# Half of the out-projection moved into the last chunk of the scan, the rest into the first iterations of the next phase, with the last two FFN contributions an iteration later

## What is computed

```python
xz = x @ W_in + b_in                        # 512 -> 2 x 1024
u, z = silu(xz[:, :1024]), xz[:, 1024:]
B, C = split(u @ W_xproj + b_xproj)         # 16 states each
dt = softplus(u @ W_dt + b_dt)
h = h * exp(dt * A) + dt * u * B;  y = sum_states(h * C) + D_param * u   # scan over time
o = (y * silu(z)) @ W_out + b_out           # the out-projection, 1024 -> 512
x = layernorm(x + o)
q = x @ wq.T + bq;  k, v from ctx (77 tokens);  16 heads of 32
x = layernorm(x + softmax(mask(q k / sqrt(32))) @ v @ wo.T + bo)
hidden = x @ W1 + b1                        # 512 -> 2048
a = relu(hidden + gain * sin(theta + 0.1 * hidden))
x = layernorm(x + a @ W2 + b2)
```

## Time and profile before

| what | value |
|---|---|
| median of 3 runs | 3416.74 us (3415.76 to 3419.22) |
| the profiled execution | 3416.91 us, span 3415.2 us |
| PE busy | 2934.8 us, 86% of the span |
| DVE busy | 2738.8 us, 80% |
| ACT busy | 1999.3 us, 59% |
| POOL busy | 1777.3 us, 52% |
| mean granted TensorE clock | 0.940 |

### The profile page before, as it was taken

How to read it: one execution, slowest core, us unless ns; L and a number is a source line. 1 busy time by engine, 2 the same in 40 slices (tenths; PEclk the granted TensorE clock), 3 DMA queues, 4 the chain that set the end, 5 groups by cost and what they waited for, 6 DMA issues and landing times. The chain is left out here.

```text
span 3415.2 us, 49521 instructions
## 1 busy us (share of the span) xinstructions
PE 2934.8 (86%) x18996; PEld 1318.5 (39%) x18996; DVE 2738.8 (80%) x3098; ACT 1999.3 (59%) x3570; POOL 1777.3 (52%) x893
## 2 busy tenths in 40 slices
PE   5888879889889888798897849999999999999997
PEld 2222222222222222222221236666666666666664
DVE  3999999999999999999999966666666666666664
ACT  4776776677667667766775444444444444444444
POOL 3797988978888879889788611111111111111100
PEclk8999999999999999999997769999999999999999
DMA  4111111111111111111113140000000000000000
GB/s 144 50 47 59 48 55 41 47 59 47 35 59 53 47 61 47 54 41 47 59 41 112 34 150 8 26 26 25 25 25 25 26 26 25 25 25 25 25 7 13
DMA packets 92547, 153.66 MB, mean 45 GB/s; under 512 B 12002, under 2 KB 29026, under 8 KB 91875
## 3 DMA queue, kind: packets, MB, share of 16 engines
q1 hardware_dynamic: 92386, 151.54, 14.0%
HBM read 92.79 MB, written 58.72 MB: 44 GB/s over the span
## 5 line engine op out<-in xcount | busy, mean ns | idle before, releaser
L722 POOL TENSOR_TENSOR h<-h,c_rep 128x1024 f32<-128x1024 f32 x512 | 1198.3, 2355 | 309.4 <-ACT carry L532 308.7
L655 DVE TENSOR_TENSOR_SCAN h<-r_ps,carry,h 128x512 f32<-128x512 f32 x768 | 942.8, 1272 | 7.2 <-ACT r_ps L526 6.5
L526 ACT ACTIVATE r_ps<-r_ps,decay 128x512 f32<-128x512 f32 x1024 | 632.0, 656 | 334.0 <-PE r_ps L295 333.3
L642 DVE TENSOR_TENSOR h<-u_ps,b_rep 128x1024 f32<-128x1024 f32 x512 | 618.7, 1208 | 44.3 <-PE u_ps L306 43.5
L1524 POOL TENSOR_TENSOR x<-x,rows 128x1024 f32<-128x1024 f32 x32 | 76.4, 2388 | 975.8 <-PE tr L961 975.8
L306 PE MATMUL u_ps<-dtu,spread 32*128 32x512 f16 x2048 | 326.6, 398 | 110.5 <-DVE h L642 109.4
L295 PE MATMUL r_ps<-dt,spread 32*128 32x512 f16 x2048 | 324.5, 396 | 75.5 <-DVE h L655 62.7
L318 PE MATMUL y_ps<-h,gather 128*32 128x512 f32 x2048 | 297.6, 650 | 55.6 <-POOL h L722 55.6
L655 DVE TENSOR_TENSOR_SCAN h<-r_ps,zero,h 128x512 f32<-128x512 f32 x256 | 313.9, 1269 | 6.9 <-ACT r_ps L526 6.7
L40 PE MATMUL nat<-region,act 128*128 128x512 f16 x512 | 206.8, 404 | 94.5 <-DVE act L1378 48.4
L40 PE MATMUL fps<-x,region 128*128 128x256 f16 x1024 | 280.9, 274 | 3.8 <-issue 2.4
(11 more groups left out here) (222 smaller groups left out, 5653.8 us busy)
## 6 DMA issues: line engine op xcount, KB each, us to landing
u_t_dram<-u SPq DMA_DIRECT2D x16, 1024.0 KB, 4.9
z_t_dram<-zs SPq DMA_DIRECT2D x32, 512.0 KB, 3.0
uz<-u_t_dram SPq DMA_DIRECT2D x64, 256.0 KB, 3.8
uz<-z_t_dram SPq DMA_DIRECT2D x64, 256.0 KB, 4.2
y_t_dram<-y SPq DMA_DIRECT2D x64, 256.0 KB, 2.4
y_t<-y_t_dram SPq DMA_DIRECT2D x15, 1024.0 KB, 7.5
x_in<-dram_x SPq DMA_DIRECT2D x16, 512.0 KB, 8.1
result<-x SPq DMA_DIRECT2D x16, 512.0 KB, 3.4
```

The source lines that it names most:

```text
L526: nc.scalar.activation(bank, bank, ACT.Exp, scale=decay[:, col:col + 1]).then_inc(s_da, 1)
L642: nc.vector.tensor_tensor(h[:, g % H_GROUPS, o:o + 2, :], u_ps[:, :, :], b_rep[:, c % 2:c % 2 + 1, :].broadcast_to([P, 2, TS]), ALU.mult). ...
L655: nc.vector.tensor_tensor_scan(row, r_ps[:, 2 * (pair % 2) + o, :], row, start, ALU.mult, ALU.add)\
L722: nc.gpsimd.tensor_tensor(rows, rows, c_rep[:, c % 2:c % 2 + 1, :].broadcast_to([P, 2, TS]), ALU.mult)\
```

## The change

**In the scan phase.** Between pairs 18 and 30 of the last chunk `W_out` is loaded and split, into the part of `region` that the u half of `W_in` has left. From pair 26 on, 16 tiles of `y_t` (tokens 0 to 2047, which were stored long before) are loaded, split, multiplied and stored to a new DRAM tensor `o`: `y_high` on ACT every second pair, `y_low` on POOL every pair, `out_piece` on PE in pairs 28 to 59, one half tile (12 matmuls of 512 columns) a pair, `evacuate_out` on ACT every second pair. The keys and values move to pairs 60 to 63.

**In the second phase.** The body takes `x1 = x + o + b_out` from DRAM loads and two POOL additions (`x1_sum`, for the next chunk), and normalizes it in the iteration before. Chunks 8 to 15 are projected here: three in iteration 0, one in each of the iterations 1 to 5, tile by tile through one `y_t` buffer, evacuated by ACT and stored to `o`. `second(6)` and `second(7)` of a chunk, its residual, layernorm and store come an iteration later (`late`), around the transposes of `x1`; so there is one body more at the end. Then come the transposes of `x2` and the queries, ahead of `hidden(0)`. The scores alternate between two lanes from matmul to matmul. POOL's `x2_bias` waits for the scores of the first tile, and `x1_sum` comes behind it. `front_back` is now called `body`, and `softmax_b` `probabilities`. The region of the split `W_1` and `W_2` is exchanged, and there are ten weight pieces to split in this phase, not twelve. Below: SP's tile loads and their places, PE's half tile, POOL's part, and the order of the bodies.

```diff
-KV_AT = (40, 42, 44, 46)
+KV_AT = (60, 61, 62, 63)
+OUT_TILES = 16
+W_OUT_AT, OUT_AT = 18, 28
...
+            def load_y_tile(i):
+                g = i % 4
+                if i < 4:
+                    sp.wait_ge(s_wol, 2 * i + 2)
+                else:
+                    sp.wait_ge(s_yl, 2 * (i - 3))
+                for r in range(2):
+                    sp.dma_start(w_out_raw[:, 2 * g + r, :].rearrange("p (q t) -> p q t", q=4),
+                                 a["y_t"].rearrange("(j p) t -> p j t", p=P)[:, 4 * r:4 * r + 4, i * P:(i + 1) * P])\
+                        .then_inc(s_yraw[g], 16)
...
+                for i in range(OUT_TILES):
+                    if s == min(W_OUT_AT + 4 + 2 * i, 62):
+                        load_y_tile(i)
+                    if s == min(OUT_AT + 2 + 2 * i, 63):
+                        store_out_tile(i)
...
+            def out_piece(i, part):
+                if part == 0:
+                    pe.wait_ge(s_oe, i) if i else pe.wait_ge(s_ev, NC * PIECES)
+                pe.wait_ge(s_yl, 2 * i + part + 1)
+                for k in range(4 * part, 4 * part + 4):
+                    tokens = slice(k % 4 * P, k % 4 * P + P)
+                    last = split_product(nc, pj[:, :], [y16[s][:, i % 4, part, tokens] for s in range(2)],
+                                         [w_out[s][:, k, :] for s in range(2)], k == 0, k == NJ - 1)
...
+                if W_OUT_AT + 2 <= s < W_OUT_AT + 2 + NJ:
+                    w_out_low(s - W_OUT_AT - 2)
+                if OUT_AT - 2 <= s < OUT_AT - 2 + 2 * OUT_TILES:
+                    y_low((s - OUT_AT + 2) // 2, s % 2)
...
+OPS_FIRST, OPS_UNTIL = 3, 6
...
+            body(0, 0, 0, True, False, False, range(OPS_FIRST), True)
+            body(1, 1, 0, True, True, False, one(1), True)
+            for c in range(2, PER_BATCH, 2):
+                two(c, 0, one if c < OPS_UNTIL else lambda c: ())
+            with e.Fori(PER_BATCH // 2, CHUNKS // 2 - 1) as h:
+                two(2 * h, 1, lambda c: ())
+            body(CHUNKS - 2, 0, 1, True, True, True, (), True)
+            body(CHUNKS - 1, 1, 1, True, True, True, (), False)
+            body(CHUNKS, 0, 1, False, True, True, (), False)
+            body(CHUNKS + 1, 1, 1, False, False, True, (), False)
```

The new body of PE (its beginning), of POOL (whole), and a piece of DVE's, in this order; ACT's order follows DVE's:

```diff
+            def body(c, par, batch, front, back, late, ops, more):
+                b, d = c - 1, c - 2
+                if late:
+                    second(d, 6)
+                if front:
+                    x1_transposed(c, par, back)
+                if late:
+                    second(d, 7)
+                if back:
+                    x2_transposed(c, par)
+                if front:
+                    queries(c)
+                if back:
+                    hidden(b, 0)
+                for m in ops:
+                    out_projection(c, m, 0)
+                    out_projection(c, m, 1)
+                if back:
+                    hidden(b, 1)
+                if front:
+                    scores(c, 0, batch, (0, 1), ops)
...
+            def body(c, par, batch, front, back, late, ops, more):
+                for m in ops:
+                    for t in range(NT):
+                        y_low(m * NT + t, t)
+                if front:
+                    x1_bias(c, par)
+                if back:
+                    pool.wait_ge(s_scp, b_scores(c, front))
+                    x2_bias(c - 1, 1 - par)
+                if more:
+                    x1_sum(c + 1, 1 - par)
...
+                if back:
                     fraction(b, 0)
+                if front:
+                    masked(c, 0, (0, 1))
+                if back:
                     fraction(b, 1)
                     mix(b, 0)
+                if front:
+                    masked(c, 0, (2, 3))
+                if back:
                     fraction(b, 2)
                     act_low(b, 0)
+                    mix(b, 1)
+                if front:
+                    row_maximum(c, 0)
+                    masked(c, 1, (0, 1))
```

More of the change, by code:

```diff
@@ L981, in hidden, with second, scores @@
                     last.then_inc(s_hp, 1)
-            def scores(c, t, batch, lanes):
+            def second(b, n, tiles=range(NT)):
+                if n == 0:
+                    pe.wait_ge(s_wlo, W2_SPLIT)
+                    pe.wait_ge(s_rw2, b * NT)
+                pe.wait_ge(s_actl, b * NU + n + 1)
+                for t in tiles:
+                    last = natural(nat[:, t, :], act16, w_2, NF, t, 2 * n, 2 * n + 2)
+                    if n == NU - 1:
+                        last.then_inc(s_w2, 1)
+            def scores(c, t, batch, lanes, ops):
                 for lane in lanes:
@@ L1078, in front_back @@
                     hidden(b, 5)
-                if front:
-                    scores(c, 1, batch, (2, 3))
-                if back:
+                    second(b, 2)
+                    hidden(b, 6)
                     second(b, 3)
-                    hidden(b, 6)
-                    second(b, 4)
-                    hidden(b, 7)
                 if front:
@@ L1458, in front_back @@
                 if back:
-                    mix(b, 1)
+                    act_low(b, 1)
                     fraction(b, 3)
-                    act_low(b, 1)
                     mix(b, 2)
+                if front:
+                    masked(c, 1, (2, 3))
+                    less_maximum(c, 0)
+                if back:
+                    act_low(b, 2)
                     mix(b, 3)
-                    act_low(b, 2)
+                if front:
+                    row_maximum(c, 1)
+                if back:
+                    fraction(b, 4)
@@ L1478, in front_back @@
                 if front:
-                    masked(c, 1, (2, 3))
-                    row_maximum(c, 1)
+                    probabilities(c, 0)
                 if back:
+                    act_low(b, 4)
                     fraction(b, 5)
-                    act_low(b, 4)
+                if front and not back:
+                    weights_low(6)
+                if more:
+                    statistics("x1", 0, c + 1, x1[:, 1 - par, :, :])
                 if front:
-                    less_maximum(c, 1)
@@ new lines, in _, with body @@
+            pool.wait_ge(s_rows, 3 * 16)
+            x1_sum(0, 0)
+            def body(c, par, batch, front, back, late, ops, more):
+                for m in ops:
+                    for t in range(NT):
+                        y_low(m * NT + t, t)
+                if front:
+                    x1_bias(c, par)
+                if back:
+                    pool.wait_ge(s_scp, b_scores(c, front))
+                    x2_bias(c - 1, 1 - par)
+                if more:
+                    x1_sum(c + 1, 1 - par)
```

736 lines of the change are left out of this document (404 added, 332 removed).

## The result

The changed kernel takes 3498.26 us (median of 4 runs, 3496.99 to 3500.74), the kernel before 3416.76 in the same comparison (4 runs): a ratio of 1.0238, with a 95% interval of 1.0221 to 1.0256. The change made the kernel 2.4% slower. The profiled execution took 3497.45 us, with a span of 3495.7, 80.5 more than before.

A forecast was written before the change was run, and what follows sets the result against it. It took DVE to bound the scan and PE the steady iteration. Its terms, +15 + 41 + 5.5 + 36 - 14 - 2 = +81.5 us on 3416.9, gave 3498 us, with a range of 3400 to 3550.

The forecast's parts named there:

- (d): Steady iteration: POOL's three operations alternate with DVE's, act_low(0) 5.8 us late, two PE waits; 84 us against 85.4.
- rival C: Steady iteration: POOL's three operations cost DVE nothing; iteration 76.5 us, total 3386; chance 0.17.
- the sentence that the prediction cited: Trainium skill on GpSimd: it contends with VectorE's instructions with two SBUF inputs or in a two-port mode.
- (c): Prologue and iteration 0: three chunks projected through one y_t buffer, 129 us in place of 88; +41, bounds +25 and +50.
- (b): Scan: added out-projection on PE, POOL's lag, and late keys and values; +15 us, bounds +4 and +35.
- POOL's lag: Scan, pairs 20 to 28: POOL has 43 us to do in 32; 5 us taken of the 11.
- (e): Iterations 1 to 5: out-projection adds 10.4 us each; +5.5 for the first, +9 for each of four.
- Iterations 6 to 15: Ten second-phase iterations without out-projection, each 1.4 us shorter than before; -14 us.
- B: Steady iteration: DVE keeps the port between operations, act_low(0) 3.6 us late; iteration 80.5, total 3446; chance 0.15.
- E: Scan becomes PE's or POOL's, tile loads late, PE's clock drops; +50 there, total 3530 to 3590; chance 0.12.
- D: Steady iteration: PE stays the bound, DVE's order costs nothing; iteration 68 us, total 3258; chance 0.04.

The follow-up runs named there:

- e1_pool_early: Changed kernel with POOL's x2_bias no longer waiting for the scores of the first tile: 3390.94 us.
- e7_one_pool_op_small: Changed kernel with POOL's addition of the out-projection's bias done for 16 of 512 columns of each row: 3470.66 us.
- e4_w_out_low_small: Changed kernel with POOL's eight w_out_low subtractions in the last scan chunk done for 16 of 512 columns each: 3497.69 us.
- e12_lows_small: Changed kernel with POOL's w_out_low and its y_low of the first four tiles done for 16 of 512 columns: 3500.53 us.
- e9_keys_values_quarter: Changed kernel with one of four contraction tiles in each keys_values step at pairs 60 to 63: 3497.44 us.
- e10_quarters_early: Changed kernel, POOL without its wait, ACT copying all four quarters of the first tile's transposed probabilities earlier, DVE's next-chunk statistics later: 3346.78 us.
- e2_probs_out_early: Changed kernel with ACT copying the first two quarters of the first tile's transposed probabilities right behind exps(c,1): 3490.74 us.
- e5_both_waits: Changed kernel with the edits of e1_pool_early and e2_probs_out_early together: 3384.6 us.
- e6_two_first: e5_both_waits with two chunks' out-projection in iteration 0 in place of three, the other six in iterations 1 to 6: 3385.81 us.

## Why the prediction was right, and where it was not

It said 3498.0 us, and 3498.26 came out. The mechanism of the steady iteration, which decides the sign, holds. That the numbers meet to 0.3 us is luck: the scan and iterations 1 to 5 came 20 us longer than predicted, and the other parts 21 us shorter.

**The iteration (d).** Right in the step that it turns on, and in the sum. Three POOL operations back to back after the fourth group of scores; they and DVE's three alternate; `act_low(0)` 5.7 us late, against 5.8 predicted; PE's wait before `second(b,0)` 5.68 us and a second one of 6.76 before the third quarter of the transposes, against 6 and 6; 83.3 to 83.9 us, against 84. Behind the last scores two slips cancel. From the last masks to the end of `fraction(6)` DVE takes 21.8 us (from 2902.64 to the end of the row below), where the prediction counted 19.2 with two `mix`, two `fraction` and no normalization of `x1`; the trace has three of each and that normalization:

```profile
2923.71 0.69 DVE L1517 TENSOR_TENSOR units<-units 128x512 f32<-128x512 f32 x1
```

From there to the end of `w_o` it is 18.4 us, where 20 and 2 for the clock were allowed. The cause of the first wait is shown by taking it away (in e1_pool_early the iteration fell to 75.1 to 76.5; rival C had 76.5 and a total of 3386, measured 3390.94) and by taking a third of it away (e7_one_pool_op_small). The changed kernel has a control of its own, though not a clean one. Iteration 15 has no next chunk, so `x2_bias` stands alone: one DVE instruction is held, PE waits 1.5 us, and the iteration takes 75.3. The next chunk's statistics and normalization are missing there as well, and the second wait is 4.1 in place of 6.8; in e1_pool_early iteration 15 is 1.4 us shorter than the one before it.
The Trainium skill (SBUF — State Buffer, Who interferes with whom) goes further than the sentence that the prediction cited: whichever of GpSimd and VectorE, with two SBUF inputs or in a two-port mode, issues first holds the shared ports for its whole instruction, and the other is fully blocked. By this rule, the traces agree: a mask instruction of 0.24 us took 2.39 in e1_pool_early. Whose turn comes next at a boundary it doesn't say; here the two alternate.

**Prologue and iteration 0 (c).** 40.2 us against 41. POOL's timeline has the first, second, third and last of the six tiles' `y_low` (the phase begins at 2002.0, as the prediction had begun it at 1974):

```profile
2036.59 2.12 POOL L1717 TENSOR_TENSOR y<-y_t,y 128x1024 f16<-128x1024 f32 x1 [19.22 <-ACT y L1308]
2043.91 2.12 POOL L1717 TENSOR_TENSOR y<-y_t,y 128x1024 f16<-128x1024 f32 x1 [5.21 <-ACT y L1308]
2054.90 3.28 POOL L1717 TENSOR_TENSOR y<-y_t,y 128x1024 f16<-128x1024 f32 x1 [8.86 <-ACT y L1308]
...
2083.25 2.13 POOL L1717 TENSOR_TENSOR y<-y_t,y 128x1024 f16<-128x1024 f32 x1 [5.26 <-ACT y L1308]
```

The first ends 36.7 us into the phase (36 predicted); then they end 7.3 to 7.7 and 12 us apart in turn, where the prediction had 9 and 11. The last matmul is at 89 (90).

**The scan (b).** The step that was mis-sized: +15, measured +27.8, inside its bounds of 4 and 35. The prediction gave POOL's lag 5 us of the 11 that it had counted, for the three groups of `h` were to take up the rest; the block in which it lies lost 12.1. POOL's work was counted rightly: from pair 20 to 28 the trace has 43.4 us (43 predicted), and the scan took 43.6 for it, in place of the 32 expected. About 4.5 of the 12.1 go with POOL's added work (e4_w_out_low_small, e12_lows_small). The rest, as far as the traces show, is a chain through PE: the piece that waits for POOL stands ahead of the next pair's replication, and after the wait it runs at half clock. The 2.6 us of the block before are a term that the prediction put at nothing: ACT's part of splitting `W_out`, ahead of the exponentials for which DVE waits. The middle blocks cost 4.3 us, where the prediction had 6 to 7 for PE less 2.5 for the keys and values that left them, and PE's 3.87 us a pair lies in the predicted 3.8 to 4.2. The last block lost 8.2 us, where it had 6; 4.7 of that are three quarters of the late steps' matmuls (e9_keys_values_quarter).

**Iterations 1 to 5 (e).** +49.0 in place of +41.5. With an out-projection an iteration takes 11.8 us more than without, not 10.4. The trace has a wait of PE that the prediction did not have, for POOL's low half of the second tile; no run takes it away, so it is not shown that the 1.4 us are this:

```profile
2439.00 0.39 PE L40 MATMUL sps<-w_out,y 128*128 128x512 f16 x1 [1.97 <-POOL y L1717]
```

**Iterations 6 to 15.** -31.9 in place of -14. Three parts: the prediction compared with 85.4 us, while iterations 6 to 14 before took 86.1 in the mean (three of them 86.7 to 87.6), 6 us; nine iterations 0.3 under 84, 3 us; and iteration 15, where `x1_sum` and the next chunk's normalization are missing, which the prediction overlooked, 9 us. It had the rule for the first of them in its hands: one POOL operation, one held instruction.

**Rivals.** B, with DVE keeping the ports, is excluded by the timeline. C needed POOL's operations to cost nothing; it is the kernel without the wait. E had the right place (POOL's scan, then PE's), at twice the price measured. D's iteration of 68 us was reached by no kernel here; e10_quarters_early came to 72.4. The 99% that D gives as PE's share is not in the rows: they have PE busy 78.8 of 85.4 us, 92%.

## What to carry to other kernels

An engine that is busy 10 us of 84 can set the pace if what it does holds another engine at a moment when a third one waits. Before a POOL operation is placed, list what DVE does beside it. In these traces instructions with one input in PSUM (1.23 us) and statistics (1.28 for two) kept their length; two-input instructions from SBUF (0.69 alone, 2.71 and 2.82 beside POOL) and the short tensor_scalars (0.42 alone, 1.96; 0.24 alone, 2.39) were each held for one POOL operation. And a wait that is removed from one step (the transposes, then `attend`) can come back at the next step that stands behind the same instruction of ACT: here moving one step won 7.5 us of 3498 (e2_probs_out_early), and moving the whole row, with DVE's statistics out of its way, 38 more than both single edits (e10_quarters_early, e5_both_waits).

Work put in the gaps of a phase that one engine bounds is not free either: ahead of an instruction on which the bound engine waits, even one piece of filler with a wait of its own can stop it. Here a piece that waited 5.4 us and ran for 4.5 kept DVE idle for 7.0.

## What the runs showed that I had not expected

POOL's operations also grew beside DVE's, from 2.35 us to 2.52 and 2.67, and 2.74 behind the short one. At the earlier place, beside DVE's PSUM-source instructions and the masks, they stayed at 2.35. And a chunk's out-projection, 10.4 us of matmuls at the higher clock, cost 11.8 us in the changed kernel's iterations, 12.5 to 13 in e1_pool_early's, 15.7 in iteration 0, and 15.9 in iteration 6 of e6_two_first. What sets the difference was not tested.
